# Perceiver block with a state-space scan and routed experts: the key bias of the attention scores moved out of TensorE's accumulation into the exponential's bias operand, and a new order at the last seam before the experts

## The reference, cut to what matters

```
x = x + xattn(layernorm(x), ctx, ctx)      # 16 batches, 64 tokens, 512 context rows
x = x + selective_scan_block(layernorm(x)) # 1024 channels, 16 states, causal conv of 4 taps
x = x + routed_experts(layernorm(x))       # 1024 tokens, 16 experts, 4 of them per token, weights 512x256 and 256x512

def xattn(Q, K, V):                        # H = 16, DK = 64
    # the reference's reshape makes 16 heads of 64 columns from a (B, T, 512) projection,
    # so that two tokens (and two context rows) share what it calls one position
    q, k, v = proj(Q, Wq, bq), proj(K, Wk, bk), proj(V, Wv, bv)
    return softmax(q @ k.T / sqrt(DK)) @ v
```

## Time and profile before

| What | Value |
|---|---|
| Median of three runs | 1383.72 us (1382.69 to 1383.88) |
| The profiled execution's own time | 1382.23 us |
| Its span in the trace | 1380.4 us |
| Busy in the span | PE 1190.3 (86%), DVE 871.5 (63%), ACT 629.5 (46%), POOL 132.5 (10%) |
| Chain that ended last | PE 60%, DVE 22%, ACT 7%, DMA 7% |
| Mean granted clock of TensorE | 0.94 |
| DMA | 266.22 MB, mean 193 GB/s |
| The preparations | about 12 to 37, 190 to 221, 441 to 481 and 675 to 714 us |
| The units | about 37 to 117, 221 to 355, 481 to 590 and 714 to 822 us |
| The last seam | about 890 to 955 us |

### The profile page before, as it was taken

The page is one execution under the profiler, slowest core; times in us unless marked ns, Lnnn a source line. Parts: engine busy times, 40 slices in busy tenths (PEclk is TensorE's granted clock), DMA queues, the critical chain, the costliest instruction groups (busy, mean ns, idle before and its releaser), DMA issues.

```text
span 1380.4 us, 13494 instructions
## 1 busy us (share of the span) xinstructions
PE 1190.3 (86%) x4404; PEld 738.6 (54%) x4404; DVE 871.5 (63%) x882; ACT 629.5 (46%) x1394; POOL 132.5 (10%) x113
## 2 busy tenths in 40 slices
PE   5996869888897899999799999835999999999993
PEld 4774745555574566666456666532444444544451
DVE  1211279655858779785897987685999993323312
ACT  4442566334356745536665563642545441222231
POOL 0010002211000006000003300011000000223002
PEclk9998989889999999999999999957999998999997
DMA  7346104999510034440013424018899993999993
GB/s 271 101 136 256 42 16 141 407 406 328 181 61 8 16 91 154 129 143 12 16 36 99 148 61 141 5 49 295 318 374 359 367 373 115 370 364 407 411 387 122
DMA packets 114038, 266.22 MB, mean 193 GB/s; under 512 B 10161, under 2 KB 43057, under 8 KB 113969
## 3 DMA queue, kind: packets, MB, share of 16 engines
q1 hardware_dynamic: 98096, 207.16, 43.3%
q0 software_dynamic: 15872, 58.20, 10.8%
HBM read 197.03 MB, written 68.29 MB: 192 GB/s over the span
## 4 chain that ended last, share of the span: by engine, by line
PE 60%; DVE 22%; ACT 7%; DMA 7%; issue 3%; POOL 1%; SPq 0%; POOLq 0%; DVEq 0%; ACTq 0%
PE bank L665 10%; PE bank L677 9%; PE bank L798 8%; PE bank L699 7%; PE bank L759 7%; DVE state L1320 6%; PE bank L819 4%; DVE state L1317 3%; PE bank L678 3%; DMA ctx<-in_ctx_t 3%; DVE state L1327 2%; DVE y_acc L1331 2%; PE bank L613 2%; PE bank L730 2%; ACT decay L1082 2%
## 5 line engine op out<-in xcount | busy, mean ns | idle before, releaser
L1320 DVE TENSOR_TENSOR_SCAN state<-decay,state 128x2048 f32<-128x2048 f32 x64 | 282.9, 4420 | 22.0 <-ACT decay L1082 21.1
L798 PE MATMUL bank<-expert_w,block_x_t 128*128 128x512 f32 x496 | 226.3, 599 | 3.0 <-ACT block_x_t L1134 2.6
L665 PE MATMUL bank<-decay,params 128*128 128x512 f32 x384 | 178.7, 610 | 5.1 <-DVE decay L1324 5.1
L1082 ACT ACTIVATE decay<-delta_even,params 128x256 f32<-128x256 f32 x256 | 107.2, 499 | 115.2 <-PE bank L665 106.7
L1611 POOL DMA_INDIRECT dispatched<-ffn_x,slot x32 | 71.0, 2218 | 796.3 <-DVE slot L1413 787.7
L677 PE MATMUL bank<-ctx,queries_ctx 128*128 128x256 f32 x512 | 133.2, 406 | 13.8 <-DMA ctx<-in_ctx_t 12.6
L798 PEld LDWEIGHTS bank<-expert_w,block_x_t 128*128 128x128 f32 x496 | 91.2, 194 | 94.6 <-issue 91.5
L1082 ACT ACTIVATE decay<-delta_odd,params 128x256 f32<-128x256 f32 x256 | 106.3, 499 | 56.8 <-PE bank L665 47.1
L699 PE MATMUL bank<-probs,ctx 128*128 128x256 f32 x512 | 121.8, 393 | 11.2 <-ACT probs L991 6.8
L699 PEld LDWEIGHTS bank<-probs,ctx 128*128 128x128 f32 x512 | 99.8, 197 | 37.6 <-issue 16.7
L819 PE MATMUL bank<-expert_w,hidden_t 128*128 128x512 f32 x248 | 117.0, 594 | 2.9 <-ACT hidden_t L1148 2.9
(11 more groups left out here) (193 smaller groups left out, 1391.8 us busy)
## 6 DMA issues: line engine op xcount, KB each, us to landing
dispatched<-ffn_x POOLq DMA_DIRECT2D x38, 1024.0 KB, 22.8
expert_w<-in_eg_t SPq DMA_DIRECT2D x62, 512.0 KB
expert_w<-in_eu_t SPq DMA_DIRECT2D x62, 512.0 KB
expert_w<-in_ed_t SPq DMA_DIRECT2D x62, 512.0 KB
ctx<-in_ctx_t SPq DMA_DIRECT2D x32, 512.0 KB, 6.9
ctx<-in_ctx_n SPq DMA_DIRECT2D x32, 512.0 KB, 4.2
bc_bcast<-bc_scratch SPq DMA_DIRECT2D x64, 256.0 KB, 5.9
block_x<-dispatched SPq DMA_DIRECT2D x62, 256.0 KB
```

Source lines behind the costliest of these rows:

```text
L665: mm = pe.matmul(y_bank[c][:, :], ident, dA[(g * NS + j) % NDEC][:, c * 512:(c + 1) * 512], start=False, stop=(j == NS - 1))
L798: mm = pe.matmul(o, xbT[q % 2][:, c, :], w_gu[q % NW][:, :, c, :], start=(c == 0), stop=(c == DC - 1))
L1082: ins = act.activation(dA[n % NDEC][:, k * gt:(k + 1) * gt], dlt[g][:, k, :], ACT.Exp, scale=par[:, c:c + 1])
L1320: dve.tensor_tensor_scan(h, dA[n % NDEC][:, 0:sw], h, 0.0, ALU.mult, ALU.add).then_inc(scan_rd, 1)
```

## The change

It does four things.

1. `scores` no longer makes the fifth product of each half. In its place `row_bias(g)` makes, once per group, 16 products of one column each (8 rows of `sb8` against a column of ones), one for each unit and half, into one bank of pair A. It stands in `attn_prep` behind the second of the four chunks c, and ahead of the sum of the first state. PE's wait for `sb8`, which stood at the end of the preparation, stands here. ACT copies the bank to `row_bias` behind its own second chunk, ahead of the decay that follows there.
2. `neg_max` on DVE has three dependent instructions in place of one: the reduction, then the row bias subtracted, then added again. The exponential takes the result as its bias. Its value is the negated maximum, up to rounding.
3. At the last seam ACT copies the transposed routed rows (`ffn_copy`, formerly the head of `ffn_logits`) ahead of the start of y and of decay 1; decays 1 and 2 stand one place later each.
4. At the last seam DVE does input product and scan of state 0, then the routing, then the rest of state 0; and slots, block table and output slots ahead of all of state 1.

```diff
@@ a_jobs
-        out += [("query_ctx", g)] * (DC * DC // 2)
+        out += [("query_ctx", g)] * (DC * DC // 4) + [("row_bias", g)] + [("query_ctx", g)] * (DC * DC // 4)
@@ tensor: attn_prep, in the loop over c
                         if mp == 0:
                             mm.then_inc(q_full, 1)
+                    if c == 1:
+                        row_bias(g)
                     if g > 0 and c in (1, 2, 3):
                         sum_state(g - 1, c - 1)
                 pe.wait_ge(q_free, (g + 1) * QPAIRS)
                 pe.wait_ge(a_free, ja.n)
+
+            def row_bias(g):
+
                 pe.wait_ge(sb8_rdy, g + 1)
+                b = job_a()
+                for k in range(NUS[g]):
+                    for qb in range(QB):
+                        mm = pe.matmul(b[:, k * QB + qb:k * QB + qb + 1], sb8[g][:, k, qb * 4:(qb + 1) * 4, :], ones8[0:H, :],
+                                       start=True, stop=True)
+                mm.then_inc(a_full, 1)
@@ tensor: scores
                     for c in range(DC):
-                        pe.matmul(o, QT[g][:, k, c, qb * P:(qb + 1) * P], ctxT[n % 2][:, c, :], start=(c == 0), stop=False)
-                    mm = pe.matmul(o, sb8[g][:, k, qb * 4:(qb + 1) * 4, :], ones8[0:H, :].to_broadcast([H, KEYS]),
-                                   start=False, stop=True)
+                        mm = pe.matmul(o, QT[g][:, k, c, qb * P:(qb + 1) * P], ctxT[n % 2][:, c, :],
+                                       start=(c == 0), stop=(c == DC - 1))
@@ scalar: attn_prep, in the loop over c
+                    if c == 1:
+                        b = job_a()
+                        act.activation(rowb[g][:, 0:NUS[g] * QB], b[:, 0:NUS[g] * QB], ACT.Copy).then_inc(a_free, 1)
+                        act.wait_ge(a_free, ja.n)
+                        act.nop().then_inc(rowb_rdy, 1)
                     if lead:
                         scan_decay(g - 1, lead.pop(0))
@@ scalar: the last seam
             scan_decay(NGR - 1, 0)
             norm_std(NTS[NGR - 2])
-            scan_decay(NGR - 1, 1)
+            ffn_copy(NGR - 2)
             y_start(NGR - 1)
             ffn_logits(NGR - 2)
+            scan_decay(NGR - 1, 1)
+            positions(NGR - 2)
             scan_decay(NGR - 1, 2)
-            positions(NGR - 2)
@@ vector: neg_max
+                add = rowb[g][:, k * QB:(k + 1) * QB]
                 dve.wait_ge(s_full, n + 1)
-                dve.tensor_reduce(...).then_inc(nm_rdy, 1)
+                step(dve.tensor_reduce(nm, bank[n % 2][:, :].rearrange("p (b k) -> p b k", b=QB), AX_X, ALU.max, negate=True))
+                if k == 0:
+                    dve.wait_ge(rowb_rdy, g + 1)
+                step(dve.tensor_tensor(nm, nm, add, ALU.subtract))
+                dve.tensor_tensor(nm, nm, add, ALU.add).then_inc(nm_rdy, 1)
@@ vector: the last seam
-            scan_step(NGR - 1, 0)
+            scan_step(NGR - 1, 0, parts=(0, 1))
             route(NGR - 2)
-            scan_step(NGR - 1, 1, parts=(0,))
+            scan_step(NGR - 1, 0, parts=(2, 3))
             slots(NGR - 2)
             block_table(0)
-            scan_step(NGR - 1, 1, parts=(1, 2, 3))
             out_slots(0)
+            scan_step(NGR - 1, 1)
```

More of the change, by code:

```diff
@@ L207, in perceiver_block @@
         rsum = sb("row_sum", 2 * QB)
+        rowb_ = sb("row_bias", 2 * NU * QB)
+        rowb = [rowb_[:, g % 2 * NU * QB:(g % 2 + 1) * NU * QB] for g in range(NGR)]
         ones8 = sb("ones", 1)
@@ L317, in perceiver_block @@
         sb8_rdy = sem("qbk_ready")
+        rowb_rdy = sem("row_bias_ready")
         q_full = sem("ctx_queries_full")
@@ L891, in norm_copy, with ffn_copy @@
                     ins.then_inc(a_free, 1)
+            def ffn_copy(c):
+                norm_copy(ffn_xT(c), NTS[c])
+                act.wait_ge(a_free, ja.n)
+                act.nop().then_inc(fxt_rdy, 1)
             def ffn_logits(c):
                 n = NTS[c]
-                norm_copy(ffn_xT(c), n)
-                act.wait_ge(a_free, ja.n)
-                act.nop().then_inc(fxt_rdy, 1)
                 b = job_a()
@@ L930, in attn_prep @@
                 if g >= 2:
+                    ffn_copy(g - 2)
                     ffn_logits(g - 2)
@@ L1163, in experts @@
                     if w == 0 and j == OUT_STEP + 1:
+                        ffn_copy(NGR - 1)
                         ffn_logits(NGR - 1)
@@ L1254, in ffn_norm, with neg_max @@
                 dve.wait_ge(fx_rdy, c + 1)
-            def neg_max(n):
+            def neg_max(g, k):
+                n = UNIT0[g] + k
+                nm = nmax[:, n % 2 * QB:(n % 2 + 1) * QB]
+                add = rowb[g][:, k * QB:(k + 1) * QB]
                 dve.wait_ge(s_full, n + 1)
-                dve.tensor_reduce(nmax[:, n % 2 * QB:(n % 2 + 1) * QB],
-                                  bank[n % 2][:, :].rearrange("p (b k) -> p b k", b=QB), AX_X, ALU.max,
-                                  negate=True).then_inc(nm_rdy, 1)
+                step(dve.tensor_reduce(nm, bank[n % 2][:, :].rearrange("p (b k) -> p b k", b=QB), AX_X, ALU.max, negate=True))
[3 more added lines that the diff above has]
+                dve.tensor_tensor(nm, nm, add, ALU.add).then_inc(nm_rdy, 1)
             def add_tiles(g):
@@ L1499, in _ @@
                     norm_stats(NTS[0], NTILES - NTS[0], mv1_, rstd1, NTS[0])
-                neg_max(k)
+                neg_max(0, k)
                 invert_sums(k)
@@ L1523, in _ @@
                         scan_step(g, now[0], parts=(0,))
-                    neg_max(n)
+                    neg_max(g + 1, k)
                     if now:
```

1 line of the change is left out of this document (added).

## The result

The changed kernel takes 1372.47 us (median, 1363.74 to 1377.52) where the kernel before, on the same chip, takes 1383.53 (1377.46 to 1386.46): a ratio of 0.9925 [0.9904, 0.9947]. It is 11 us faster, not 22.9; the forecast of 1360.8 is missed, and the range of 1351 to 1374 holds the time near its upper end. The profiled execution, 1377.52 us with a span of 1375.8, is the slowest of its runs, so its rows show some 5 us more than the median, and the two spans lie only 1380.4 - 1375.8 = 4.6 us apart. The mean granted clock of TensorE fell, from 0.940 in the profile before to 0.924.

What follows compares the result with a forecast made beforehand. It took PE to bound groups 0, 2 and 3 and the clears' DMA group 1. Terms -7.9 + 5.0 - 9.0 - 9.0 - 2.0 = -22.9 us gave 1360.8 us; 8-in-10 range 1351 to 1374.

Steps and rivals of the forecast that it cites:

- Product removed: Scores on PE: without the fifth product of each half a unit loses 1.55 us, bounds 1.26 and 1.6.
- Products added: Row bias on PE: 32 one-column passes a group at 0.12 us each, 3.8 us; upper end 13.8 us.
- The idle time of 3.4 us: Group 1's preparation: PE waits 3.4 us for ACT's copy ahead of the row bias, so the sum starts 7.2 us later.
- Group 0: Stall of 4.5 us in the preparation against 12.4 us gained in eight scores: net -7.9 us.
- Group 1: First scores 5.6 us later, then bound by the clears' bytes, hiding PE's gain: net +5.0 us, bounds +7.2 and -3.
- Groups 2 and 3: The 7.2 us delay about made up by the end of the first scores, six other units give 9.3: net -9.0 us each.
- The maximum: Two more dependent instructions on DVE cost 0.40 us a unit, covered by PE in groups 2 and 3.
- the cover of 0.6 us: Groups 2 and 3: DVE's work of 10.3 us a unit stays under PE's 10.9, with 0.6 us left of 2.4.
- The seam: Last seam: earlier routing and slots end the dispatch 0.9 to 3.2 us earlier; net -2.0 us, bounds 0 and -4.
- The rival that held: Preparations: small products and ACT's wait cost more, clock falls in the idle gap; 3 to 5 us a group, about 1375; 18%.
- The estimate of 3.4 us: Row bias on PE: 32 weight loads a group priced by columns, so eight rows give no rebate: 3.4 us.

Runs made afterwards that it cites:

- the run with one product: Changed kernel with a single product a group at the row bias's old place, in place of 16: 1352.77 us, ratio 0.9764 to the kernel before.
- the block of 64 behind the sum: Changed kernel with each row-bias product made twice and the block placed behind the first state's sum: 1384.48 us, ratio 1.0005 to the kernel before.
- the key bias alone: Changed kernel with the last seam's order as before, so only points 1 and 2 of the change: 1376.81 us, ratio 0.9949 to the kernel before.
- two lines of order: Changed kernel with the first state's sum put ahead of the row-bias products on PE: 1350.11 us, ratio 0.9807 to the kernel before.

## Why the prediction was wrong

- **Product removed: right.** 1.65 us a unit in groups 0 and 2 against 1.55. The units of groups 0, 2 and 3 lose 11.7, 14.5 and 12.4 us against 12.4.
- **Products added: the step that failed.** "I take 3.8" holds at full clock only; behind the sum they take 3.73. At their place they take 5.6 to 6.5 us, and the half clock costs what follows another 2.1 to 3.0. So the term was 17.7 us for the four groups, and the runs without the products put it at 35 to 39. The row that I priced them by the earlier trace rows was at full clock, while the same operation in the earlier trace rows took 3.57 us at half clock for 16 passes. The idle time of 3.4 us that I had worked out myself was there, 3.48; I charged its length and not its effect on the clock. The experiments show both causes: the gap (the run with one product, groups 1 to 3) and the block itself (the block of 64 behind the sum, and group 0).
- **Group 0: wrong.** +10.4 in the preparation where I had +4.5, or +7.2 in the profile of the key bias alone. The chunks behind the products run at half clock. Net -1.4 in the one profile and -3.8 in the other, in place of -7.9.
- **Group 1: right in size by luck, wrong in path.** +12.0 in the preparation where I had 7.2, -13.6 in the units where I had next to nothing, +8.0 in the rest where I had none: +6.4 against +5.0. I had the bytes as the bound of the units; they are the bound of units and rest together, since the broadcasts for the last states share the DMA engines.
- **Groups 2 and 3: wrong.** -6.6 and -1.5 against -9.0 each, by the same term: 12.0 us ahead of the second chunk's sum, of which DVE's wait (2.54) and the half clock behind it (1.7) are saved, which leaves 7.8 and not 3.0. In group 3 another 3.2 us stand ahead of the gap, where nothing was changed: the mean granted clock from the second half of the queries to the gap is 0.79, against 0.93 before over the same work.
- **The maximum: right.** The scan stands 1.00 us behind the reduction, 0.39 more than before. DVE has 10.16 us of work a unit against PE's 10.78, so the cover of 0.6 us held, and the run without products but with the additions is no slower than the one without them.
- **The seam: right.** -3.8 us in its own run (1.4 to 6.2) and 2.7 us at the first expert block, against -2.0.
- **The rival that held** is the first, small products and clock in every group, at 18% and 1375; the measured median lies 2.5 us below it. The argument against it (a half clock in groups 2 and 3 "is already in the time before") covered 1.7 us in two of four groups. In groups 1 to 3 it held by the gap and the block together, in group 0 by the block alone, which the rival did not say. The rule of the Trainium skill that stood behind it (TensorE: Matmul & The Clock Gate, HAM oscillation), on gaps between bursts, agrees with the run with one product. It does not cover the block behind the sum, where the clock fell with no gap ahead. The estimate of 3.4 us from the load formula of the Trainium skill (TensorE: Matmul & The Clock Gate, LDWEIGHTS) lies 9% below the 3.73 at full clock, and no clock stood in it.

What stays open: group 0's preparation, with the same work in it, takes 31.4 us in one profile (the key bias alone) and 34.6 in another (the changed kernel). The mean granted clock over it is 0.89 in the one and 0.80 in the other (1.00 in the kernel before), which goes with the difference; why the clock stood low for longer, also ahead of the products, no run shows, nor why it did so in group 3. And the products at a place where PE has nothing to do in group 0 weren't tried.

## What to carry to other kernels

Price a block of small products at the clock of the place where it will stand: an idle gap ahead of it, or its own length, takes the clock down, and what stands behind pays as well. If a product needs a bank that another engine is still copying, put long independent products between; here two lines of order were worth 16 to 22 us, more than the whole change. When a stage is bound by DMA, look for idle DMA time ahead of it before shortening the engines' work in it.

## What the runs showed of the hardware

- Passes with one column, each with its own weight load, start 0.117 us apart at a granted clock of 1.0 (32 in 3.73 us) and about 0.2 us apart mostly at 0.5 (64 in 13.17 us); 32 columns cost the same as one (24.3 against 24.0 us for the 128 passes of the program).
- TensorE's granted clock fell from 1.0 to 0.5 (2.4 to 1.2 GHz) inside a block of such passes with no idle time before it (1.00, 0.76, 0.50 in three windows of 2 us, 64 passes in 9.53 us). Behind an idle gap of 3.48 us it fell 0.7 us into a block of 64 and stayed down to its end (13.17 us). It also fell behind the same gap with one product in place of the block (the sum took 5.40 us and not 3.70), and did not fall with one product behind a gap of 0.89 us.
- Two dependent additions on 128x2 between a reduction and a scan put the scan 0.39 us later. They moved the program's time by nothing that its runs can tell, where DVE had 10.16 us of work a unit under PE's 10.78.
